# Keys' loads moved to the front of a step, score tiles of one bank in a ring of three, and a ring of four for maxima and small products

## What is computed

```python
latent = x @ Wc_down
q = (latent @ Wq_up).reshape(Bsz, Tlen, N_HEAD, HEAD_DIM)      # 16 heads of 8
kv = latent @ Wkv_up
k, v = (kv[..., :HEAD_DIM], kv[..., HEAD_DIM:])                # one k and v for all heads
att = jnp.einsum('bthd,bsd->bhts', q, k) * scale
att = jnp.where(causal[None, None], att, -jnp.inf)
att = jax.nn.softmax(att, axis=-1)
y = jnp.einsum('bhts,bsd->bthd', att, v).reshape(Bsz, Tlen, C)
return y @ Wc_proj
...
h = _layernorm(x, axis=-1) * (1 + ca) + sa
x = x + ga * _L0_attn_ref(h, L0_attn_Wc_down, L0_attn_Wq_up, L0_attn_Wkv_up, L0_attn_Wc_proj)
h = _layernorm(x, axis=-1) * (1 + cb) + sb
x = x + gb * _L0_ffn_ref(h, L0_ffn_Wr, L0_ffn_W1, L0_ffn_b1, L0_ffn_W2, L0_ffn_b2)
```

## Time and profile before

| | |
|---|---|
| median of 3 runs | 889.79 us (885.54 to 890.29) |
| profiled execution | 883.99 us, its span 882.2 us |
| busy share of the span | PE 83%, DVE 64%, ACT 51%, POOL 45% |
| rounds 0 to 7 of the first attention | from 77.7 us to about 376 us of the span |
| mean granted clock of TensorE | 0.907 of full speed |

### The profile page before, as it was taken

How to read it: one execution, slowest core, us unless ns; L and a number is a source line. 1 busy time by engine, 2 the same in 40 slices (tenths; PEclk the granted TensorE clock), 3 DMA queues, 4 the chain that set the end, 5 groups by cost and what they waited for, 6 DMA issues and landing times.

```text
span 882.2 us, 22943 instructions
## 1 busy us (share of the span) xinstructions
PE 730.6 (83%) x9158; PEld 384.5 (44%) x9158; DVE 561.2 (64%) x1506; ACT 450.2 (51%) x742; POOL 400.6 (45%) x531
## 2 busy tenths in 40 slices
PE   4588896999898898948889978899947699999887
PEld 2234343444444443323334434444424356556555
DVE  4877675878686775466763423302287688888884
ACT  2013664666575657713225423333346588888663
POOL 5021022524233232210036888887545669885333
PEclk9756998999999999969999978899957799999999
DMA  6621454256543432230011333333300111111001
GB/s 164 130 56 32 96 153 98 58 124 178 103 97 92 96 80 72 79 105 39 0 26 45 43 40 44 45 45 33 50 25 2 25 27 25 38 26 26 18 22 37
DMA packets 73924, 55.06 MB, mean 62 GB/s; under 512 B 23699, under 2 KB 66819, under 8 KB 73219
## 3 DMA queue, kind: packets, MB, share of 16 engines
q1 hardware_dynamic: 63098, 36.58, 16.3%
q0 software_dynamic: 9856, 7.58, 6.7%
q10 hardware_dynamic: 864, 9.44, 5.1%
HBM read 31.76 MB, written 18.23 MB: 57 GB/s over the span
## 4 chain that ended last, share of the span: by engine, by line
PE 42%; DVE 19%; DMA 12%; issue 7%; POOL 6%; SPq 6%; ACT 5%; another core or an unknown queue 1%; POOLq 1%; DVEq 0%; ACTq 0%
PE ps_o L1585 6%; DMA d_r<-rc 4%; PE bank L462 3%; PE b1ps L2075 3%; PE b1ps L2086 3%; PE ps_s L423 3%; DVE R L1477 3%; PE bank L439 3%; DVE MX L798 3%; POOL d_acc L1381 3%; PE ps_h L1573 3%; DMA K<-d_k 2%; PE b1ps L2099 2%; POOL xn L983 2%; SPq L1088 2%
## 5 line engine op out<-in xcount | busy, mean ns | idle before, releaser
L798 DVE TENSOR_REDUCE MX<-bank 128x1 f32<-128x320 f32 (+13 forms) x352 | 180.8, 562 | 56.6 <-PE bank L469 54.2
L649 ACT ACTIVATE PR<-ps_s 128x1024 f32<-128x1024 f32 x160 | 155.7, 1022 | 107.7 <-PE ps_s L419 65.5
L462 PE MATMUL bank<-K,Q 72*32 72x32 bf16 (+15 forms) x2048 | 122.6, 314 | 37.6 <-DMA K<-d_k 23.3
L462 PEld LDWEIGHTS bank<-K,Q 72*32 72x32 bf16 x2048 | 49.6, 106 | 125.4 <-DVE MX L798 60.1
L423 PE MATMUL ps_s<-Q,K 97*32 97x512 bf16 (+1 forms) x1088 | 96.1, 386 | 5.6 <-DMA Q<-d_m 4.7
L1381 POOL DMA_INDIRECT d_acc<-Y,idx x56 | 87.7, 1566 | 20.7 <-issue 16.2
L1371 POOL DMA_INDIRECT XG<-d_tab,idx x56 | 53.9, 963 | 78.2 <-DVE idx L1486 60.6
L439 PE MATMUL bank<-PR,VE 128*32 128x512 f32 x640 | 87.6, 625 | 0.0
L1585 PE MATMUL ps_o<-H,w 128*128 128x512 f32 x176 | 86.4, 641 | 0.0
L1705 ACT ACTIVATE H<-ps_h,b1T 128x512 f32<-128x512 f32 x88 | 60.3, 687 | 43.9 <-PE ps_h L1573 31.4
L469 PE MATMUL bank<-maskQ,identb 128*32 128x32 bf16 (+3 forms) x1408 | 73.3, 201 | 0.0
(11 more groups left out here) (347 smaller groups left out, 1375.7 us busy)
## 6 DMA issues: line engine op xcount, KB each, us to landing
Q<-d_q ACTq DMA_DIRECT2D x24, 384.0 KB
d_q<-qs SPq DMA_DIRECT2D x24, 128.0 KB, 2.7
X<-L_attn_x SPq DMA_DIRECT2D x8, 256.0 KB, 5.0
w<-L_ffn_W SPq DMA_DIRECT2D x8, 256.0 KB, 4.3
d_acc<-zrow SPq DMA_DIRECT2D x1, 2048.0 KB, 11.2
w<-L_ffn_W SPq DMA_DIRECT2D x1, 2048.0 KB, 9.7
AC<-d_acc SPq DMA_DIRECT2D x8, 256.0 KB, 3.0
d_y<-ysb SPq DMA_DIRECT2D x112, 18.0 KB
```

What stands on the lines that cost most here:

```text
L462: nc.tensor.matmul(mx[o:o + QW, x * w:(x + 1) * w], Q[b % QB][0:NPR, 4 * c + hh, QW * j:QW * j + QW], K[b % QB][0:NPR, 0:w], start=(x == 0 ...
L649: nc.scalar.activation(by_head.rearrange("p h (c x) -> p c h x", x=QW), ps_s[half][:, :].rearrange("p (c h x) -> p c h x", c=2, x=QW), ACT ...
L798: nc.vector.tensor_reduce(MX[b % 2][:, c:c + len(cs)], ring[R0.place["max", G]][:, 0:len(cs) * w].rearrange("p (x w) -> p x w", w=w), AX_X ...
```

## The change

Three edits come together. In SP's program the loads of k stand in front of the reciprocals' piece in step 4. The score tiles become three tiles of one bank, one for each of the four slots in turn, and ACT takes four exponentials of 512 columns in a step where it took two of 1024. The bank that this frees (4 + 2 x 2 banks before, 5 + 3 now) goes to the ring of maxima and small products, which now has four. Each score tile waits for the exponential three tiles before it. At the start, the rows of the modulation, which used the score tiles, use three of them and a part of `ps_y`, and DVE copies them in four pieces where it copied two.

```diff
-NRING = 3
+NRING = 4
+NSB = 3
...
-    bank = [a0.enter_context(nc.psum_tensor(f"bank{i}", [P, 512], F32)) for i in range(4)]
-    ps_s = [a0.enter_context(nc.psum_tensor(f"ps_s{i}", [P, 1024], F32)) for i in range(2)]
-    ring, ps_y = bank[0:3], bank[3]
+    bank = [a0.enter_context(nc.psum_tensor(f"bank{i}", [P, 512], F32)) for i in range(5)]
+    ps_s = [a0.enter_context(nc.psum_tensor(f"ps_s{i}", [P, 512], F32)) for i in range(NSB)]
+    ring, ps_y = bank[0:3] + bank[4:5], bank[3]
...
-            t2 = 2 * (NSTEP * b + s) + half
-            if t2 >= 2:
-                pe.wait_ge(S["exp_done"], t2 - 1)
+            u = NT * (NSTEP * b + s) + j
+            if u >= NSB:
+                pe.wait_ge(S["exp_done"], u - NSB + 1)
...
-            pe.wait_ge(S["exp_done"], 2 * t + 2)
+            pe.wait_ge(S["exp_done"], NT * t + NT)
...
-                    if x < 2 and 0 <= n < NB:
+                    if 0 <= n < NB:
                         scores_T(n, s, x)
...
-                    for half in range(2):
-                        act.wait_ge(S["sT_full"], 2 * t + half + 1)
+                    for j in range(NT):
+                        act.wait_ge(S["sT_full"], NT * t + j + 1)
...
-                lk(nc.vector.tensor_copy(modR[:, l, :].rearrange("b (h f) -> b h f", h=2),
-                                         ps_s[l][0:NB, :].rearrange("b (h f) -> b h f", h=2)[:, :, 0:384]))
+                for h in range(2):
+                    lk(nc.vector.tensor_copy(modR[:, l, 384 * h:384 * h + 384], mod_rows[2 * l + h]))
...
+                b = n + 2
+                if 0 <= b < NB and s == 4:
+                    par = b % 2
+                    sp.wait_ge(DS[f"k_st{par}"], 64 * (b // 2 + 1))
+                    for c in range(PARTS):
+                        sp.dma_start(K[b % QB][24 * c:24 * c + 24, :],
+                                     bass.AP(d_k[par].tensor, c * DH * T, [[0, PARTS], [T, DH], [1, T]])
+                                     ).then_inc(DS[f"q_in{par}"], 16)
                 if 0 <= t - 1 < NSTEP * NB:
                     b, ps = divmod(t - 1, NSTEP)
                     g, i = STEPS[ps]
...
-                b = n + 2
-                if 0 <= b < NB and s == 4:
-                    par = b % 2
-                    sp.wait_ge(DS[f"k_st{par}"], 64 * (b // 2 + 1))
-                    for c in range(PARTS):
-                        sp.dma_start(K[b % QB][24 * c:24 * c + 24, :],
-                                     bass.AP(d_k[par].tensor, c * DH * T, [[0, PARTS], [T, DH], [1, T]])
-                                     ).then_inc(DS[f"q_in{par}"], 16)
```

More of the change, by code:

```diff
@@ L165, in __init__ @@
             if u in late:
-                k = NRING - 1
+                k = 2
             else:
@@ L349, in program @@
     R0 = Ring(ring_order())
+    mod_rows = [ps_s[i][0:NB, 0:384] for i in range(NSB)] + [ps_y[0:NB, P:P + 384]]
     M0 = Misc([u for u in ring_order() if u[0] != "max"], 1)
@@ L388, in modulation @@
                 for h in range(2):
-                    last = nc.tensor.matmul(ps_s[l][0:NB, h * 512:h * 512 + 384], siluT[:, l, :],
+                    last = nc.tensor.matmul(mod_rows[2 * l + h], siluT[:, l, :],
                                             wmod[:, l, h * 384:(h + 1) * 384], start=True, stop=True)
@@ L401, in acquire, with scores_T @@
                 pe.wait_ge(S["misc_free"], M0.full(ahead))
-        def scores_T(b, s, half):
+        def scores_T(b, s, j):
             g, i = STEPS[s]
-            if b == 0 and s == 0 and half == 0:
+            if b == 0 and s == 0 and j == 0:
                 pe.wait_ge(s_modR, 2)
-            if s == 0 and half == 0:
+            if s == 0 and j == 0:
                 pe.wait_ge(DS[f"m_in{b % 2}"], 48 * (b // 2 + 1))
-            t2 = 2 * (NSTEP * b + s) + half
-            if t2 >= 2:
-                pe.wait_ge(S["exp_done"], t2 - 1)
+            u = NT * (NSTEP * b + s) + j
+            if u >= NSB:
+                pe.wait_ge(S["exp_done"], u - NSB + 1)
             q_, k_ = Q[b % QB], K[b % QB]
[L413 to L425, removed]
+            for kt in range(NT):
+                o = QW * kt
+                out_ = ps_s[u % NSB][o:o + QW, :]
+                if i == g and kt > j:
+                    last = nc.tensor.matmul(out_, maskT[:, QW:2 * QW], bc(identb[:, 0:1], [P, 512]),
+                                            start=True, stop=True, tile_position=(0, o))
+                else:
+                    r = P if i == g and kt == j else KF
+                    last = nc.tensor.matmul(out_, k_[0:r, P * i + o:P * i + o + QW],
+                                            q_[0:r, :, P * g + QW * j:P * g + QW * j + QW],
+                                            start=True, stop=True, tile_position=(0, o))
             last.then_inc(S["sT_full"], 1)
@@ L647, in scalar_part @@
                         by_head = PR[t % 2][:, :, :].rearrange("p a (l q) -> p (a l) q", q=P)
-                        by_head = by_head[:, :, 2 * QW * half:2 * QW * half + 2 * QW]
-                        nc.scalar.activation(by_head.rearrange("p h (c x) -> p c h x", x=QW),
-                                             ps_s[half][:, :].rearrange("p (c h x) -> p c h x", c=2, x=QW), ACT.Exp,
+                        nc.scalar.activation(by_head[:, :, QW * j:QW * j + QW],
+                                             ps_s[(NT * t + j) % NSB][:, :].rearrange("p (h x) -> p h x", x=QW), ACT.Exp,
                                              scale=DH ** -0.5).then_inc(S["exp_done"], 1)
```

## The result

The changed kernel takes 903.59 us (median of 4 runs, 896.82 to 906.46), the kernel before 887.66 us (4 runs, 883.99 to 890.29). The ratio is 1.0203, 95% interval 1.0156 to 1.025. The prediction said 888 us, 877 to 897. The profiled execution of the changed kernel took 906.46 us, its span 904.7 us; rows of it are set against those of before's 883.99 us.

What follows compares the result with a forecast made beforehand. It took a round as a chain through PE, DVE and two DRAM trips, no engine full. +12.5 - 2.0 - 7.8 + 2.0 - 0.7 - 0.8 - 0.2 - 1.0 = 2.0 us won: 888 us against the median 889.79, range 877 to 897.

Steps and rivals of the forecast that it cites:

- +12.5: SP's chain: issue time of k's loads saved, 2.5 us a round over five rounds, 12.5 us won.
- -2.0: Reciprocals' store behind three more issues in SP's queue: lands 0.4 us later, five times, 2.0 us lost.
- their landing then comes at about that of q, 216.43 + 8: k's loads issued beside q's: landed at 224.4, before PE asks at 227.44, so k's wait goes in rounds 2 to 5.
- The rule on packets in turn: DMA engines alternate between queues, so k's and q's packets don't hurry each other; speaks against early k, counted as nothing.
- -7.8: Fourth scores in slot 3: ACT issues q's loads 1.3 us later in six rounds, 7.8 us lost.
- +2.0: DVE's 1.2 us longer wait for q's copy and the fourth bank's lead: together 0.3 us won in seven rounds.
- The exponentials: ACT's four of 512 for two of 1024: 0.2 us more a step, hidden in rounds 0 to 6, -0.7 in round 7.
- The terms for rounds 6 and 7, the start and the clock: Late exponentials in round 7 -0.7, `Q<-d_m` wait in round 6 -0.8, modulation copies -0.2, low clock from new waits -1.0 us.
- (b): Rival: ACT's late q loads and DVE's longer wait for q's copy decide; 7 us slower, 897 us, chance 0.24.
- (a): Rival: transfers gain more, ACT's later issue is hidden and PE's path decides; some 10 us won, 880 us, chance 0.37.
- (c): Rival: q's later loads become step 8's wait in all rounds, nothing won; 890 us, chance 0.10.

Runs made afterwards that it cites:

- k_first: The kernel before with only k's loads moved ahead of the reciprocals' piece in SP's step 4; ratio 1.0032 to the kernel before.
- k_mid: The kernel before with k's loads between the reciprocals' store and the wait for its landing; ratio 0.9916 to the kernel before.
- q_early_2: The changed kernel with only q's loads ahead of ACT's fourth exponential of step 4, copies still behind it; ratio 1.0035 to the kernel before.
- act_early_2: The changed kernel with ACT's fourth exponential of a step behind its copies and q's loads; ratio 0.9960 to the kernel before.
- ring3_slots01_2: The changed kernel with k's loads at their old place, two score tiles each in slots 0 and 1, and a ring of three; ratio 1.0040.
- slots01_only: The changed kernel with k's loads at their old place and two score tiles each in slots 0 and 1, ring of four; ratio 1.0023.
- slots_only: The changed kernel with k's loads back at their old place; ratio 1.0176 to the kernel before.
- act_early_k_mid: The changed kernel with ACT's fourth exponential behind its copies and q's loads, and k's loads between reciprocals' store and landing wait; ratio 0.9869.

## Why the prediction was wrong

**"+12.5" for k's loads off SP's chain, "-2.0" for the reciprocals' store.** This pair forecast 10.5 us won; k_first measured 0.3% lost, some 3 us. The step that failed is "it can land 0 to 1.5 us later against the end of q's loads, and I take 0.4": the reciprocals' load went out 4.1 us later against q's loads (11.8 for 7.6 us). I had read the store's 7.3 us as bound to the end of q's packets, and had only asked what SP does next, not who waits for the reciprocals: POOL's `yn` and PE's product behind it (L501). That wait is not in the earlier trace rows, as it was 0, and I gave it no margin. The cause is shown by one pair: with the loads behind the store (k_mid) the wait for `yn` is 2.1 us and 0.8% is won, with the loads ahead of it (k_first) 11.3 us and nothing. The step "their landing then comes at about that of q, 216.43 + 8" failed as well: k's loads issued beside q's were there 12.3 us (changed) and 222.71 - 211.10 = 11.6 us (k_first) behind q's issue, and 12.5 us when issued 8 us later.

**The rule on packets in turn.** I had quoted the Trainium skill, "DMA: Bandwidth & Descriptors", section "Queues, rings and completion order", for engines that take packets in turn from the queues. The rows between 232 and 235 us show both queues served, as the rule has it, but at 0.39 MB to 0.03; the small packets beside the large ones did not finish early. That it spoke against an early k was right, and I should have let it into the sum.

**"-7.8" for q's loads 1.3 us later.** The lateness was as forecast in kind and larger in size (2.5 us from hT's transposes, 1.7 from the round's first scores: 20.74 for 19.09 us). Its price was mis-sized by half: 1.3 us of it, taken away in six rounds by q_early_2, gave back 15 us, not 7.8. Why a late load costs about twice its lateness is not shown; a lower clock in the rounds (0.89 to 0.93) goes with it.

**"+2.0" for DVE's longer wait and the fourth bank together.** This was the wrong sign. The copies' lateness costs some 6.6 us (act_early_2 against q_early_2), the bank gave nothing measurable (ring3_slots01_2 against slots01_only). I had DVE's wait right (1.2 us longer forecast, 1.1 measured at L748) and left out that the bank of q stays full as long: a fourth bank that an undrained product holds gives no lead. The same holds for hT's bank, which I didn't price.

**How the pieces add up.** 1.0032 (k_first) and 1.0176 (slots_only) give 1.0208 together, and the change measured 1.0203. But 3, 15 and 6.6 us are 25 us, and the loss is 16: the last two prices are taken from act_early_2's 0.9960, which lies below k_first. The single prices are good to some us, and their order is what is shown.

**Smaller terms.** The exponentials, in slots01_only's groups by form (count, busy us, mean ns, idle before):

```profile
L649 ACT ACTIVATE PR<-ps_s 128x512 f32<-128x512 f32 x320 | 165.7, 602 | 93.9 <-PE ps_s L419 63.9 <-PE ps_s L423 29.4
```

602 ns each, as taken, but 165.7 us together, where 320 x 0.602 = 192.6: neighbours overlap, and 160 of 1024 took 155.7. The 10 us more of ScalarE in all rounds cost nothing that this kernel's ratio shows. The terms for rounds 6 and 7, the start and the clock, 2.7 us together, were not measured apart. For the clock I had less than I wrote: the wait of 1.35 us that I set beside round 3's lower clock lies at the end of round 2's window, whose clock is 1.00.

**The rivals.** (b) had the right mechanism, "ACT's lateness decides", with a chance of 0.24 and 897 us. Its point of decision, a copy and q's issue over 2 us late together, was passed: 1.1 and 1.7 to 2.5 us. It came out 7 us too low and still counted 10.5 us for SP; without them it would have said 907 us. (a) needed ACT's later issue to be hidden, and it isn't. (c) didn't occur: no wait for `Q<-d_q` in the changed kernel.

Of what I named to look for, SP's issue beside ACT's (0.3 us), the later loads of q and DVE's 1.36 us came; the end of the waits for k, the one for `Q<-d_q`, the waits for `Q<-d_m` at the starts of rounds 5 and 6 (that of round 2 was 0.2 us) and rounds of 38 to 40 us did not.

## What to carry to other kernels

Before a producer is moved to a later slot, list what stands behind its consumer in the other engine's program: here, in one step or another, the copies of y, hT, q and k and three DMA issues stood behind one exponential, and putting that exponential last, or its scores earlier, took back 2%. Here a small transfer issued behind a bigger one landed with the bigger one and not by its own issue time (9.0 us, for 1.5 us just ahead of it), so try the store whose landing somebody awaits first, and what is needed later behind it. A large sum of short waits (46.2 us here) is not by itself a reserve: the fourth bank took some 20 us of it away (32.0 to 11.4 us) and no time was won.

## What the runs showed of the hardware that I had not expected

The profiled executions fall into two groups behind round 6. From L496 of that round to the end of the span it takes 542.7 us in the kernel before, in the changed one, in act_early_2 and in q_early_2, and 543 to 544 in the other two of that session; in all profiles of the first and third sessions it takes 552 to 557 us. Most of the difference arises in one stretch of some 25 us in the experts' stage, where ACT's copies wait for something that the trace has no name for ("remote"). k_mid, then act_early_2 at the same place:

```profile
450.42 0.78 ACT L1722 ACTIVATE YD<-ps_o,b2g,gbT 128x512 f32<-128x512 f32 x1 [7.34 <-remote]
457.49 0.78 ACT L1722 ACTIVATE YD<-ps_o,b2g,gbT 128x512 f32<-128x512 f32 x1 [6.29 <-remote]
460.32 0.49 ACT L1736 ACTIVATE WT<-ps_l 128x384 f32<-128x384 f32 x1 [2.05 <-remote]
```

```profile
452.73 0.78 ACT L1722 ACTIVATE YD<-ps_o,b2g,gbT 128x512 f32<-128x512 f32 x1 [7.09 <-PE ps_o L1589]
457.23 0.78 ACT L1722 ACTIVATE YD<-ps_o,b2g,gbT 128x512 f32<-128x512 f32 x1 [3.73 <-PE ps_o L1589]
457.91 0.48 ACT L1736 ACTIVATE WT<-ps_l 128x384 f32<-128x384 f32 x1
```

In k_mid PE then stood 11.0 us for ACT's next copy. The kernel before was slower in the same sessions (892.47 and 893.12 us for 882.78), so it goes with the session more than with the kernel. But the third session holds a gap of this kind within one kernel: act_early_k_mid took 872.4 to 876.5 us in three runs and 882.9 to 884.3 in three, of which the profiled one is one of the longer. So the ratios of that session may carry a part of it, and their intervals are wide. And a comparison of two single spans can mislead: k_mid's (881.8 us) beside that of before (882.2 us) shows no gain, where the ratio gives 0.8%. The cause stays open.
